# Bank sets, opening steps, stage places and the high part's cast in a gated Toeplitz convolution kernel

## The reference, cut to what matters

```
x: (8, 64, 64, 96) fp32;  D1 = 288 channels in 8 heads
xn = x / (norm(x) / sqrt(96) + eps)                 # over the 96 channels
u  = silu(xn @ u_w.T + u_b);   v = silu(xn @ v_w.T + v_b)
out = tno(v, rows, network 2) + tno(v, columns, network 1)
return (u * out) @ o_w.T + o_b + x

tno(v, axis, network):      # length n = 64 along the axis
    a = network(positions 0..63, 0, -63..-1)        # 1 -> 256, three layers 256 -> 256, -> 288
    return convolution of v with a along the axis   # by FFT of length 128
network layer: h = relu(h / rms(h)) @ w.T + b
```

## Time and profile before

| what | value |
|---|---|
| median of 3 runs | 787.2 us (786.3 to 788.52) |
| profiled execution | 789.24 us, span 787.4 us |
| TensorE busy | 751.0 us, 95% of the span |
| ScalarE, VectorE, GpSimd busy | 534.5, 473.4, 280.6 us |
| mean granted clock of TensorE | 0.983 of full |
| DMA | 161.12 MB, 205 GB/s |

### The profile page before, as it was taken

How to read it: one execution, slowest core, us unless ns; L and a number is a source line. 1 busy time by engine, 2 the same in 40 slices (tenths; PEclk the granted TensorE clock), 3 DMA queues, 4 the chain that set the end, 5 groups by cost and what they waited for, 6 DMA issues and landing times.

```text
span 787.4 us, 19301 instructions
## 1 busy us (share of the span) xinstructions
PE 751.0 (95%) x7178; PEld 678.7 (86%) x7178; DVE 473.4 (60%) x858; ACT 534.5 (68%) x868; POOL 280.6 (36%) x187
## 2 busy tenths in 40 slices
PE   6699999998999999899999999998999999899997
PEld 5599989997999999799999999997999999787785
DVE  7566645336788898444444444444555544488887
ACT  3366667765666676677777777774766676676674
POOL 4333333211311122455555555511000000398885
PEclk8799999999999999999999999999999999999999
DMA  8655555479888976588888988859555555499996
GB/s 196 153 162 161 161 164 159 154 203 212 177 194 181 197 169 162 156 259 268 272 272 267 271 272 265 269 189 203 142 133 135 135 136 135 161 281 316 322 325 197
DMA packets 132306, 161.12 MB, mean 205 GB/s; under 512 B 69772, under 2 KB 97420, under 8 KB 132236
## 3 DMA queue, kind: packets, MB, share of 16 engines
q1 hardware_dynamic: 132236, 160.15, 73.3%
HBM read 109.49 MB, written 50.63 MB: 203 GB/s over the span
## 4 chain that ended last, share of the span: by engine, by line
PE 83%; DMA 6%; DVE 5%; issue 2%; ACT 2%; POOL 1%; SPq 1%; ACTq 0%; DVEq 0%; POOLq 0%
PE ps L1004 25%; PE ps L1093 16%; PE ps L1065 10%; PE ps L1078 9%; PE ps L1014 8%; PE ps L1024 8%; PE ps L995 3%; DMA x_e<-in_x_eT 3%; DMA stage<-a_dram 2%; PE ps L1027 1%; DVE g L906 1%; DVE x_e L915 1%; POOL u_in L515 1%; DMA u_in<-u_dram 1%; PE ps L978 1%
## 5 line engine op out<-in xcount | busy, mean ns | idle before, releaser
L515 POOL TENSOR_TENSOR u_in<-u_in,v 128x1152 f32<-128x1152 f32 (+2 forms) x66 | 174.7, 2655 | 156.0 <-DMA u_in<-u_dram 138.5
L906 DVE TENSOR_TENSOR g<-ps,g 128x512 fp32r<-128x512 f32 (+1 forms) x192 | 125.4, 679 | 50.2 <-ACT g L582 41.4
L862 DVE COPY toepB<-stage 64x512 f32<-64x512 f32 x144 | 105.4, 732 | 79.2 <-PE ps L1093 69.5
L1093 PE MATMUL ps<-toepB,vt 128*128 128x128 f32 x1152 | 141.3, 276 | 0.0
L1093 PEld LDWEIGHTS ps<-toepB,vt 128*128 128x128 f32 x1152 | 136.0, 194 | 0.2 <-issue 0.2
L1004 PE MATMUL ps<-wu,xh 97*128 97x288 f32 x512 | 124.7, 309 | 2.2
L1004 PE MATMUL ps<-wv,xh 97*128 97x288 f32 x512 | 120.6, 311 | 4.7 <-DVE xl L771 3.7
L771 DVE TENSOR_TENSOR xl<-ps,xh 96x512 fp32r<-96x512 f32 x64 | 43.9, 686 | 127.9 <-ACT xh L555 127.8
L559 ACT ACTIVATE v<-ps 128x576 f32 (+1 forms) x128 | 83.5, 652 | 43.4 <-PE ps L1004 33.1
L1014 PE MATMUL ps<-ident,u_in 128*128 128x128 f32 (+1 forms) x768 | 101.3, 275 | 5.0 <-POOL u_in L515 4.5
L1024 PE MATMUL ps<-g,wo 128*96 128x512 f32 x384 | 101.9, 400 | 0.0
(11 more groups left out here) (83 smaller groups left out, 1021.2 us busy)
## 6 DMA issues: line engine op xcount, KB each, us to landing
stage<-a_dram SPq DMA_DIRECT2D x144, 256.0 KB, 4.3
u_in<-u_dram SPq DMA_DIRECT2D x64, 576.0 KB, 5.5
u_dram<-u_out SPq DMA_DIRECT2D x48, 576.0 KB, 3.3
x_e<-in_x_eT SPq DMA_DIRECT2D x64, 192.0 KB, 4.3
out<-x_e SPq DMA_DIRECT2D x64, 192.0 KB, 4.1
u_dram<-u_in SPq DMA_DIRECT2D x16, 576.0 KB, 3.1
x_n<-in_x SPq DMA_DIRECT2D x16, 384.0 KB, 5.9
xa<-in_x SPq DMA_DIRECT2D x64, 96.0 KB, 4.6
```

What stands on the lines that cost most here:

```text
L515: return nc.gpsimd.tensor_tensor(out=tile, in0=tile, in1=v[:, start // 2:end // 2, bass.ds(t * NB, NB)].rearrange("p c n e -> p n c e"), o ...
L862: nc.vector.tensor_copy(toepB[n % 2][rows, :, rows], stage[n % STAGES][rows, axis].rearrange("p k c -> p c k")[:, :, ::-1]).then_inc(toepB ...
L906: nc.vector.tensor_tensor(out=low, in0=ps[0:w, bank], in1=high.bitcast(f32), op=ALU.subtract).then_inc(gl_ready, 1)
L1093: last = nc.tensor.matmul(ps[:, SET_BANK[n % 2] + c // NB, (c % NB) * P:(c % NB + 1) * P], vt[n % 2][:, c], toepB[n % 2][:, c], start=Fals ...
```

## The change

- **Three sets of banks.** In half 0 the pairs go round three sets, banks 0, 1 then 2, 3 then 4, 5 (`pair_banks`), and a pair waits for the SiLU of three pairs before. Half 1 keeps two sets.
- **One bank for the networks.** All of their products use bank 7 (`R_BANK`). The sums of squares are taken with one column of ones instead of 128. The last layer is split: network 0's result at r = 3 of chunk 3, network 1's at r = 0 of chunk 4, after the first has been copied.
- **Opening.** The positions' weights are loaded ahead of x. Steps 0 and 1 (`FIRST` = 2) are loaded, squared on VectorE and normed as one batch, steps 2 and 3 as the next. The networks' first squares and sums come ahead of them. The low parts of the weights move from VectorE to GpSimd. In steps 0 and 1 the next step's transposes stand between pairs 1 and 2, and ScalarE's cast between the SiLUs of v and u. The warming transposes become 12, 34 and 8 in place of 30.
- **High part on VectorE.** From chunk 5 on (`HIGH_FROM`) the cast of the high part is VectorE's.
- **Stage places.** Half 0 uses places 0, 1 and 3, half 1 places 0, 1 and 2. All three first stages of half 0 are loaded in phase A. The fourth and fifth stages stand ahead of the first reload of u and the first load for the norms; the norms of half 1 move one unit later. In half 1 u tile 3 is loaded ahead of the others.
- **Last unit.** Its two crossing copies are VectorE's, and in half 0 stand ahead of `low_x` of step 32. In half 1 TensorE transposes two thirds of step 0 before that unit is copied out.

```diff
-        stage = [place(f"stage{k}", [P, 2, H, UNIT], V + U_BYTES * k) for k in range(STAGES)]
+        STAGE_PLACES = ((0, 1, 3), (0, 1, 2))
+        A_SETS, R_BANK = 3, 7
+        def pair_banks(half, t, pair):
+            return 2 * ((PAIRS * t + pair) % A_SETS if half == 0 else pair % 2)
...
-            engine.wait_ge(conv_out, Y_PARTS * (UNITS * half + unit + 1))
+            before = half * (Y_PARTS * (UNITS - 1) + 1)
+            if unit < UNITS - 1:
+                engine.wait_ge(conv_out, before + Y_PARTS * (unit + 1))
+            else:
+                engine.wait_ge(conv_out, before + Y_PARTS * unit + 1)
+                engine.wait_ge(conv_crossed, 2 * (half + 1))
...
-            def project(xs, r, pair):
+            def project(half, xs, r, pair):
                 pe.wait_ge(xl_ready, xs + 1)
-                wait(pe, silu_done, PAIRS * xs + (pair - 1))
+                wait(pe, silu_done, PAIRS * xs + pair + 1 - (A_SETS if half == 0 else 2))
...
+            warm(WARM[0])
+            pe.wait_ge(zeroed, 2)
+            rpe_sums(0)
+            warm(WARM[1])
             transpose_x(0, 0)
+            warm(WARM[2])
...
                 for r in range(CH):
                     t = CH * c + r
+                    opening = first and r < FIRST
+                    if not opening and not (last and r == CH - 1):
                         transpose_x(t + 1, r + 1)
+                    if c <= LAYERS and r == 0 and c:
+                        rpe_sums(c)
+                    if c <= LAYERS and r == 2:
+                        rpe_spreads(c)
+                    if c < LAYERS and r == 3:
+                        rpe_layers(c)
+                    if c == LAYERS and r == 3:
+                        rpe_result(0)
+                    if c == LAYERS + 1 and r == 0:
+                        rpe_result(1)
+                    for pair in range(PAIRS):
...
+                        project(0, t, r, pair)
+                        if opening and pair == 1:
+                            transpose_x(t + 1, r + 1)
...
+            def high_x(xs, r, bank=X_BANK):
+                dve.wait_ge(x_transposed, xs + 1)
+                dve.wait_ge(projected, PAIRS * (xs - 1))
+                nc.vector.tensor_copy(xh[r % 2][0:E], ps[0:E, bank]).then_inc(xh_ready, 1)
...
+            run(opening[:9])
+            low_x(1, 1)
+            run(opening[9:])
...
+                        if not isinstance(c, int) or c >= HIGH_FROM:
+                            high_x(CH * c + (r + 1), r + 1)
                         low_x(CH * c + (r + 1), r + 1)
...
                 if half == 0:
                     set_x_rows(0)
+                dve.wait_ge(conv_done, UNITS * (half + 1))
+                n = UNITS - 1
+                for i in range(2):
+                    to, of = slice(H * i, H * i + H), slice(H - H * i, P - H * i)
+                    nc.vector.tensor_copy(v[to, UNIT // 2 * n + UNIT // 4:UNIT // 2 * (n + 1)],
+                                          ps[of, SET_BANK[n % 2] + 1].rearrange("p (c e m) -> p c m e", e=2, m=P)
+                                          ).then_inc(conv_crossed, 1)
+                if half == 0:
                     low_x(STEPS, 0)
```

More of the change, by code:

```diff
@@ new lines, in rpe_spreads, with rpe_layers @@
+            def rpe_spreads(layer):
+                pe.wait_ge(rpe_diag, 2 * (layer + 1))
+                for n in range(2):
+                    last = nc.tensor.matmul(ps[:, R_BANK, n * P:(n + 1) * P], r_ones[:], r_diag[:, n],
+                                            start=True, stop=True)
+                last.then_inc(rpe_spread, 1)
+            def rpe_layers(layer):
+                if layer == 0:
+                    pe.wait_ge(rpe_loaded, RPE_LOADS * 16)
+                pe.wait_ge(rpe_normed, RC * (layer + 1))
+                for n in range(2):
+                    for o in range(RC):
@@ new lines, in rpe_layers, with rpe_result @@
+                last.then_inc(rpe_layer, 1)
+            def rpe_result(n):
+                pe.wait_ge(rpe_normed, RC * (LAYERS + 1))
+                wait(pe, a_ready, n)
+                for c in range(RC):
+                    nc.tensor.matmul(ps[:, R_BANK, 0:D], r_in[:, n, c], rows(OW + NCH * (RC * n + c), NCH, E),
+                                     start=(c == 0), stop=False)
+                nc.tensor.matmul(ps[:, R_BANK, 0:D], r_ones[0:1], rows(OB + NCH * n, NCH, E, slice(0, 1)),
+                                 start=False, stop=True).then_inc(rpe_layer, 1)
```

276 lines of the change are left out of this document (128 added, 148 removed).

## The result

The changed kernel takes 776.4 us, the kernel before 786.8 us beside it on the same chip (medians of four runs each; 775.5 to 780.7 and 784.7 to 788.5). The ratio is 0.988, 95% interval 0.984 to 0.992: faster, by 10.3 us. The prediction said 766.8 with a range of 760.0 to 775.5. The sign was right, the size was half of what was forecast, and the measured time lies 0.9 us outside the range.

A forecast was written before the change was run, and what follows sets the result against it. TensorE, with 83% of the chain that ended last, was taken as the bound. Terms 4.3 + 3.8 + 7.3 + 4.5 - 1.5 + 2.0 = 20.4 us off 789.24 gave 768.8, median 766.8; range 760 to 775.5.

The forecast's parts named there:

- Three sets of banks: Half 0 projections from chunk 4: the 0.27 us hole per step, blamed on ScalarE's cast, goes; 4.3 us gained over sixteen steps.
- The cast on VectorE: Projections from chunk 5: the cast takes 0.65 us on VectorE, covered by about 1.8 us of slack; cost nothing.
- The networks in one bank: Chunks 1 to 3: holes and sums save 1.3 + 0.3, 0.35 returns as a wait; 1.25 a chunk, 3.8 us in all.
- The sums with one column: Networks' sums of squares in chunks 1 to 3: streaming one column instead of 128 saves 0.3 us a chunk.
- The opening: Start of the half 0 projections: chunk 1 begins at 38.75 instead of 46.04, despite a low clock; 7.3 us gained.
- Into the first convolution: Seam from projections to half 0's convolution: of 5.1 us lost to late third and fourth stage loads, 4.5 regained.
- Out of it: Seam after half 0's convolution: VectorE's low part now stands behind two copies, delaying the gate's transposes; 1.5 us lost.
- Into the last stretch: After half 1's convolution: earlier transposes of step 0, GpSimd's gate and u loads; 2.0 us gained.
- the rival about the DMA queue: Last stretch: the DMA queue sets its time, so the 2.0 us gain is lost whole; 769 us, chance 0.07.
- From the sum to the median: Whole kernel: the forecast for the profiled execution, 768.8 us, lowered by 2.0 to the median, 766.8.
- the hole isn't the bank wait: Projection steps: the 0.27 us hole comes from the change from wv to wu, three sets do nothing; 775 us, chance 0.06.
- Openings pay less: Opening, networks and seam into the convolution gain only 5, 2.5 and 2.5 us; about 772 us, chance 0.22.

The follow-up runs named there:

- the run with all edits: Changed kernel plus GpSimd squares later, scale factors first, third stage and u load later, low part first, second convolution's stages one by one: 761.3 us.
- the kernel whose opening has no such idle time: Changed kernel with all helpful edits, and the first two stores of u issued ahead of the load of x of chunk 3: 758.6 us, ratio 0.964.

## Why the prediction was right or wrong, step by step

- **Three sets of banks** (4.3; bounds 3.5 to 4.6). Right in size: 3.62 a step instead of 3.64, 0.29 gained. Wrong in its reason, which made ScalarE's cast the culprit; the run with two sets shows that the cast was not in the way, and the SiLU's own 0.65 does not fit beside one pair.
- **The cast on VectorE** (0). Right; it takes 0.69 us there (0.65 was taken), nothing waits for it, and it gains nothing either.
- **The networks in one bank** (3.8; bounds 2.5 to 5). Wrong, 1.4 with the step behind them (of which that step is 0.3). The step that failed is "some 0.35 comes back as a wait". The prediction saw the chain and that TensorE already waited 0.21 for it, and then let the wait grow by the hole of one step. But nearly all that TensorE saves ahead of r = 2 comes back there (the wait is 0.33 to 0.36 with two sets, 1.23 to 1.37 with three), as the chain's second half hangs on a cast and ends with 1.7 us of two instructions held by GpSimd. The wait grew by 1.0 to 1.2. The gain was to be had by turning two instructions round (17.8 a chunk).
- **The sums with one column.** Eight passes take 0.81 us from the first to the next instruction (36.21 to 37.02), 0.10 each. The chain had shown 0.89 for 128 columns, but measured alike they took 0.81 too, in the kernel before:

```profile
46.31 1.06 PE L962 MATMUL ps<-r_ones,free_rows 128*128 128x128 f32 x8
47.12 0.38 PE L1004 MATMUL ps<-wv,xh 97*128 97x288 f32 x1
```

The saving was nothing, not 0.3. The rule cited, the Trainium skill, TensorE: Matmul & The Clock Gate, "Wait — 56ns, not 53.3ns?", would have made it 0.2 us for the eight; the trace goes against its use here. The Trainium skill's same page gives in "LDWEIGHTS (loading the stationary operand)" the time of a weight load in ns as its columns divided by 1.2, an estimate of 107 ns for 128 columns, and the trace is near that (0.10 us a pass). Each pass has its own weight load of 128 columns, and the eight loads take 0.97 us in both kernels, so the moving columns do not show.
- **The opening** (7.3; bounds 5 to 10). The mechanism was right to 0.1 us at the transposes of step 3 (the first projection came at 14.57, 1.0 later than forecast, which the wait for GpSimd hid). The clock was not: after 2.99 us of idle time it stayed at its upper level in this execution and fell in six others. The forecast of 38.75 is what the run with two sets shows (39.0); 35.8 is the best of eight.
- **Into the first convolution** (4.5; bounds 2.5 to 4.9). Wrong, a loss of 0.6, and the largest miss. The old waits went, as forecast. The prediction asked what is late next among the stages, and found only the sixth, with 1 us to spare; it came 1.35 late. It did not ask who stands behind the third stage load in the queue: the store of step 29, for which the last SiLUs and with them TensorE wait. It moved the load past that store and costed it at nothing. Nor did it reckon that shorter steps bring the end nearer to that store. 2.57 idle, 1.7 of slower clock and 1.35 at unit 6 are 5.6, against 5.1 before.
- **Out of it** (a loss of 1.5; 0.8 to 2.5). Right: 2.0.
- **Into the last stretch** (2.0; bounds 0.5 to 3.3). Wrong, 0.1. The transposes do go earlier, but then TensorE waits 1.31 and 1.95 us, where it waited 2.51 once. It waits for GpSimd's gate of step 1, 2.7 us, which can begin only when the last unit is copied out, in both kernels. Only 0.5 came through to the first product (8.07 against 8.60 us), and the rest of the stretch gave 0.4 back (98.4 against 98.0). Whether the full DMA engines did that, as the rival about the DMA queue has it, no run tells. The prediction counted the gate of step 0 and left that of step 1 out. No run removed this gate, so this rests on the trace alone.
- **The second convolution** lost 1.0 us that no term had: a lower clock for longer after an idle time that was alike (3.62 and 3.73). Nine other profiles with the same instructions at that place (one of them of the kernel before) show 5.3 to 5.6 six times, 6.5 twice and 4.0 once, this last behind 3.31 us of idle time and at full clock, and so the 1.0 is not the change's.
- **From the sum to the median.** The forecast took the profiled execution's distance to the median (2.0) as fixed. The profiled execution of before lay 2.5 above its median here, that of after 0.1 below its own, so 12.9 in the trace are 10.3 in the medians.

Of the rivals, "the hole isn't the bank wait" came nearest in number (775), which is luck, since the hole did go. "Openings pay less" (772) had two of its terms on the right side, the networks (2.5; 1.1 measured) and the seam (2.5; a loss of 0.6), but not its opening. The rival about the cause of the hole was wrong, yet so was the forecast's own cause.

## What to carry to other kernels

When a load is moved ahead in a queue, list what it is now in front of, and find the engine that waits for each: a store that frees a buffer is as critical as a load. When TensorE's steps become shorter, follow the serial chain that it waits for instead of adding the saved holes up; if the chain hangs on a fixed event, everything saved ahead of the wait is lost there. And in such a chain put the instructions that others wait for ahead of the one that wakes an engine which competes with them.

## What the hardware showed that was not expected

- The same two VectorE instructions (`r_diag`, 128x128 each) take 0.49 us with GpSimd still and 1.71 beside its scalings.
- Eight passes with one moving column and a new load of 128 columns of weights each take 0.81 us, and 0.81 with 128 moving columns.
- An idle time of 2.1 to 3.2 us ahead of step 3's transposes brought the lower clock in six profiles (granted clock 0.72 to 0.84 from 22 to 30 us) and not in a seventh (2.99 us idle, 1.00). In the worst case, behind 2.67 us of idle time in the run with all edits, it stayed at 0.52 of full, all but wholly at 1.2 GHz, for 13 us although TensorE was busy 12.50 of them. What decides it stays open. The six executions of the kernel whose opening has no such idle time lie within 5.3 us; one of them was profiled, at 1.00.
